# The last stage of a fused decoder kernel: expert slots worked out and filled in two halves, and a tail by batch that stores the output itself

## The reference, cut to the last stage

```python
h = _layernorm(x, ln_g, ln_b).reshape(Tn, D)            # Tn = 1024, D = 128
top_vals, top_idx = jax.lax.top_k(h @ Wr, 2)            # 7 routed experts
gates = jax.nn.softmax(top_vals, axis=-1)
idx, gat = top_idx.T.reshape(-1), gates.T.reshape(-1)   # all first picks, then all second picks
tok = jnp.tile(jnp.arange(Tn), 2)
onehot = jax.nn.one_hot(idx, 7, dtype=jnp.int32)
pos = jnp.sum(jnp.cumsum(onehot, axis=0) * onehot, axis=-1) - 1
keep = pos < CAPACITY                                   # 366
pos_c = jnp.where(keep, pos, CAPACITY)
xe = jnp.zeros((7, CAPACITY, D)).at[idx, pos_c].set(h[tok], mode='drop')
ye = einsum(silu(einsum(xe, W1)) * einsum(xe, W3), W2)  # per expert, 512 wide inside
out_slots = ye[idx, clip(pos_c)] * (gat * keep)[:, None]
routed = jnp.zeros((Tn, D)).at[tok].add(out_slots)
shared = (silu(h @ W1s) * (h @ W3s)) @ W2s
x = _layernorm(x + routed + shared)                     # the kernel's output
```

## Time and profile before

| what | us |
|---|---|
| median of 3 runs (lowest, highest) | 2411.19 (2404.15, 2413.72) |
| the profiled execution's own time | 2407.47 |
| its span, first to last instruction | 2405.6 |
| last stage within it | 2251.8 to 2405.6 |
| PE busy over the span | 2038.5 (85%) |
| mean granted PE clock over the span | 0.906 |

### The profile page before, as it was taken

How to read it: one execution, slowest core, us unless ns; L and a number is a source line. 1 busy time by engine, 2 the same in 40 slices (tenths; PEclk the granted TensorE clock), 3 DMA queues, 4 the chain that set the end, 5 groups by cost and what they waited for, 6 DMA issues and landing times. The chain is left out here.

```text
span 2405.6 us, 59384 instructions
## 1 busy us (share of the span) xinstructions
PE 2038.5 (85%) x24530; PEld 1251.5 (52%) x24530; DVE 1331.8 (55%) x3370; ACT 1129.3 (47%) x2591; POOL 969.7 (40%) x868
## 2 busy tenths in 40 slices
PE   4988999869976899999999999999769756699773
PEld 2445666635543555565555555555535545355452
DVE  3545554447725776767776767776236423465322
ACT  1333445115523676767676767676415211145221
POOL 2010000011215887878787878787110133100123
PEclk8999999879968999999999999999769767889887
DMA  2110000000002021211111212121000032100411
GB/s 66 24 36 1 1 1 1 1 18 3 3 1 72 18 60 27 47 39 42 40 47 35 60 27 51 36 48 24 14 14 7 1 110 89 27 2 2 132 39 40
DMA packets 70558, 78.47 MB, mean 33 GB/s; under 512 B 10608, under 2 KB 48634, under 8 KB 70291
## 3 DMA queue, kind: packets, MB, share of 16 engines
q1 hardware_dynamic: 64098, 61.75, 9.9%
q0 software_dynamic: 3696, 10.56, 1.5%
q10 hardware_dynamic: 2496, 2.36, 0.4%
HBM read 40.90 MB, written 6.82 MB: 20 GB/s over the span
## 5 line engine op out<-in xcount | busy, mean ns | idle before, releaser
L3490 POOL TENSOR_TENSOR l1fb_rinv<-l1fb_ssq,neghalf 128x8 f32<-128x8 f32 x192 | 316.2, 1647 | 159.5 <-DVE l1fb_ssq L3533 157.0
L3633 ACT ACTIVATE l1fb_p<-ps,l1fb_shift 128x64 f32<-128x64 f32 x768 | 177.7, 315 | 158.7 <-PE ps L3789 137.8
L3492 POOL TENSOR_TENSOR l1fb_qk<-l1fb_qk,l1fb_r 128x512 f32<-128x512 f32 x192 | 244.5, 1273 | 0.0
L3696 PE MATMUL ps<-l1fb_wqkv,l1fb_xs 128*128 128x512 f32 x384 | 219.5, 655 | 10.3 <-DVE l1fb_r L3543 6.2
L3494 POOL TENSOR_TENSOR l1fb_qk<-l1fb_qk,l1fb_rinv 128x512 f32<-128x512 f32 x192 | 200.4, 1044 | 15.1
L3543 DVE TENSOR_TENSOR l1fb_r<-ps,l1fb_turn_tab 128x256 f32<-128x256 f32 x384 | 143.0, 414 | 0.0
L3540 DVE TENSOR_TENSOR l1fb_qk<-ps,l1fb_turn_tab 128x512 f32<-128x512 f32 x192 | 132.4, 690 | 14.4 <-POOL l1fb_qk L3492 12.5
L3531 DVE TENSOR_REDUCE l1fb_ssq<-l1fb_sq 128x8 f32<-128x512 f32 x192 | 129.8, 676 | 3.0 <-ACT l1fb_sq L3613 3.0
L3613 ACT ACTIVATE l1fb_sq<-ps 128x512 f32<-128x512 f32 x192 | 118.7, 618 | 11.9 <-PE ps L3696 11.2
L3727 PE MATMUL ps<-ident,l1fb_qk 128*128 128x128 f32 x768 | 116.6, 275 | 5.7 <-POOL l1fb_qk L3494 2.5
L3641 ACT ACTIVATE l1fb_both<-ps 128x512 f32<-128x512 f32 (+1 forms) x194 | 117.3, 605 | 8.3 <-PE ps L3789 7.7
(11 more groups left out here) (722 smaller groups left out, 4773.8 us busy)
## 6 DMA issues: line engine op xcount, KB each, us to landing
l1fb_v<-l1fb_v SPq DMA_DIRECT2D x48, 260.0 KB, 4.2
l1fb_v<-l1fb_v SPq DMA_DIRECT2D x48, 195.0 KB, 4.0
l1fb_wqkv<-in_L_ffn_Wqkv SPq DMA_DIRECT2D x24, 256.0 KB, 2.8
l3f_w<-in_L_ffn_W SPq DMA_DIRECT2D x21, 256.0 KB, 6.5
l1fb_wqkv<-in_L_ffn_Wqkv SPq DMA_DIRECT2D x6, 512.0 KB, 4.7
l1fb_wo<-in_L_ffn_Wo SPq DMA_DIRECT2D x6, 512.0 KB, 4.1
l1fb_w<-in_L_ffn_W SPq DMA_DIRECT2D x6, 341.0 KB, 3.0
l3f_xs<-zeros SPq DMA_DIRECT2D x1, 1344.0 KB, 6.9
```

The lines of the kernel that those rows point to most:

```text
L3490: nc.gpsimd.tensor_tensor(w.rinv[:, u, :], w.ssq[:, u, :], chip.neghalf[:, 0:8], ALU.pow).then_inc(*w.unit_norm.end(f"rinv{u}"))
L3492: nc.gpsimd.tensor_tensor(w.qk[:, u, :], w.qk[:, u, :], fp(w.r2), ALU.add).then_inc(*w.unit_norm.end(f"add{u}"))
L3633: last = nc.scalar.activation(w.p[:, c % 2, q, j, :], ps[:, SCORE_BANK + j, q * SEEN:(q + 1) * SEEN], ACT.Exp, bias=w.shift[:, c, j, q:q + 1])
L3696: nc.tensor.matmul(ps[:, PROJ_BANK(u), :], w.xs[:, x.odd, q * P:(q + 1) * P], w.wqkv[:, col:col + 512], start=True, stop=True)\
```

## The change

It touches `l3_ffn` and the last block of the program only.

1. **Gate.** The 1024 columns of `hT` are made in two halves, the first by DVE once 4 tiles have been turned, the second by ACT. The logits of the first 4 tiles wait for the first half alone. The clearing of the two PSUM banks moves to the head of PE's list, ahead of everything.
2. **Counts.** PE counts first picks as soon as they exist, and second picks after those, two matmuls of 56 columns each time; both stand ahead of the shared expert's first piece.
3. **Placing** is a function `placed(s)`, called for first picks (s = 0) and second picks (s = 1). The 15 successive additions are replaced by three additions over 63 columns (each tile with the one 1, 2 and 4 places before it) on a padded tile `run`, which POOL sets to zero. The second half adds the first half's total. `placed(0)` stands ahead of `mixed(0)`, `placed(1)` between `mixed(0)` and `mixed(1)`.
4. **Scatter.** POOL issues the 8 scatters of first picks when `sent0` is there, the other 8 after `sent1`.
5. **Tail.** DVE adds residual and shared result once (`kepty`, 1024 columns) before the gathers land; it then takes each batch from gathered rows to variance when they arrive. POOL raises the first three batches together (6 columns) and the last alone. All eight normalisations stand at the end of DVE's list, six and then two.
6. **Output.** SP stores three batches after the six, the last batch after the two, within the stage's own block; the extra block is gone.

```diff
+            nc.gpsimd.memset(fp(run), 0.0).then_inc(*rpool.end("runs"))
             eng.wait_ge(*emptied.of(0))
-            eng.wait_ge(*cdve.done("sent"))
             for i in range(2 * TILES):
+                if i % TILES == 0:
+                    eng.wait_ge(*cdve.done(f"sent{i // TILES}"))
                 nc.gpsimd.indirect_dma_start(xs, ...)
...
+            def placed(s):
+                at = slice(s * TILES, (s + 1) * TILES)
+                bank = (5, 4)[s]
+                n = TILES
+                a0, a1 = run[:, 0, s, :, :], run[:, 1, s, :, :]
+                eng.wait_ge(*cpe.done(f"counts{s}"))
+                eng.wait_ge(*rpool.done("runs"))
+                nc.vector.tensor_copy(a0[:, n + 1:2 * n + 1, :], ps[:, bank, S:S + n * E]...)
+                for src, dst, step, before, name in ((a0, a1, 1, "run", "two"), (a1, a0, 2, "two", "four"), (a0, a1, 4, "four", "eight")):
+                    eng.wait_ge(*cdve.done(f"{before}{s}"))
+                    nc.vector.tensor_tensor(dst[:, n:2 * n + 1, :], src[:, n:2 * n + 1, :], src[:, n - step:2 * n + 1 - step, :], ALU.add)
...
+            placed(0)
             mixed(0)
-            totals = ps[:, 5, S:S + 2 * TILES * E].rearrange("p (i e) -> p i e", e=E)
-            for i in range(1, 2 * TILES):
-                nc.vector.tensor_tensor(offs[:, i, :], offs[:, i - 1, :], totals[:, i - 1, :], ALU.add)
-                if i == TILES:
-                    mixed(1)
...
+            placed(1)
+            mixed(1)
             mixed(2)
...
+            nc.vector.tensor_tensor(fp(kepty), ps[:, 6:8, :]..., x_tiles, ALU.add).then_inc(*bdve.end("kept"))
...
+            for which, part in (("", range(0, TILES - QT)), ("_last", range(TILES - QT, TILES))):
+                eng.wait_ge(*bpool.done("rstd" + which))
+                for q in part:
+                    last = nc.vector.tensor_scalar(x_tiles[:, q, :], mixedy[:, q, :], ymv[:, q, 0:1], yroot[:, q:q + 1], ALU.subtract, ALU.mult)
+                last.then_inc(*bdve.end("normed" + which))
...
+            sp.wait_ge(*bdve.done("normed"))
+            sp.dma_start(batch(0, B - 1), chip.x_tok[:, 0:B - 1, :, :]).then_inc(written, 16)
+            sp.wait_ge(*bdve.done("normed_last"))
+            sp.dma_start(batch(B - 1, 1), chip.x_tok[:, B - 1:B, :, :]).then_inc(written, 16)
+            sp.wait_ge(written, 32)
...
-        stored = ctx.enter_context(nc.semaphore("stored"))
-        with nc.Block() as block:
-            @block.sync
-            def _(sp):
-                sp.dma_start(out.rearrange("b (t p) d -> p b t d", p=P), fp(chip.x_tok)).then_inc(stored, 16)
-                sp.wait_ge(stored, 16)
```

163 lines of the change are left out of this document (96 added, 67 removed).

## The result

The changed kernel took **2395.66 us** (median of 11 runs, 2388.5 to 2403.1), the kernel before 2413.36 us beside it (11 runs). The ratio is **0.9927, 95% interval 0.9908 to 0.9946**: 17.6 us less, 13 to 22 by the interval.

What follows compares the result with a forecast made beforehand. Bound: the last stage's path of gate, placing, 16 scatters, load, experts, store, gathers, tail, output. 9.8 + 4.6 = 14.4 us off 2407.47 gives 2393.1, plus 3.7 for the median 2396.8; predicted between, 2395.5, range 2388 to 2403.

Steps and rivals of the forecast that it cites:

- Gate: Gate in halves at the start of the last stage: logits end 1.5 us earlier.
- Placing and scatter: First picks' destinations ready 9.8 us earlier, second picks' with 4.6 us of cover; last scatter ends 9.8 us earlier.
- scatters are held up beside the weights: Scatter stream stands until 2276.5 while the weights load: loss 5.5 us, gain 8.9, time 2401; chance 0.10.
- The clears: PSUM clearing on PE (3.78 us), moved to the stage's start, ends before `z` is there: free.
- The sum: 9.8 us up to the last scatter plus 4.6 us in the tail: 14.4 us saved.
- Experts and clock: PE waits 3.8 to 4.7 us for the first expert's rows; same expert instructions, 64 us; clock falls again.
- The rival with the clock: Clock stays up through the shortened wait ahead of the experts: up to 2.6 us more, time 2393; chance 0.22.
- The cover of 4 us: PE's slack between the shared expert's end and the first expert's rows: 3.8 to 4.7 us, where there were 13.7.
- a sign of being wrong: Ahead of the routed experts: wrong if PE is still on the shared expert when the rows arrive.
- Tail: After the last gather: last normalisation 1.8 us closer, then 3 us to the end instead of 5.9; 4.6 us saved.
- the rule that I weighed: In the tail, DVE's normalisations could shut POOL out of a shared port pair: end about 1 us later.
- the rival of a weaker tail: A block's end costs the same wherever it stands: gain 12.1 or 11.4 us, time 2398; chance 0.11.

Runs made afterwards that it cites:

- four scatters: Changed kernel with only four of the 16 scatters, the loads of the experts' rows waiting for the fourth; stage 131.7 us.
- front: Kernel before with the change's gate, counts, placing and scatters by halves, old tail and output; ratio 0.9988 (0.9966 to 1.0009).
- tail: Kernel before with the tail by batch and the stores in the stage, old gate and placing; ratio 0.9997 (0.9984 to 1.0010).
- after, again: Changed kernel run once more without edit, against the kernel before; ratio 0.9953 (0.9936 to 0.9970), stage 141.4 us.
- both additions: Changed kernel with clears behind the logits, three unread matmuls at stage start, five ahead of the first expert; ratio 0.9937 (0.9918 to 0.9957).
- after: Changed kernel in its first timing, against the kernel before; 2395.66 us, ratio 0.9927 (0.9908 to 0.9946).
- start only: Changed kernel with three unread matmuls at stage start in place of the clears, which go behind the logits; ratio 0.9944 (0.9923 to 0.9965).
- front, again: Kernel before with only gate, counts, placing and scatters by halves, timed a second time; ratio 0.9956 (0.9939 to 0.9972).

## Why the prediction was right, point by point

**Gate.** Logits end 12.15 us from the stage's start instead of 13.55: 1.4 us earlier, forecast 1.5. DVE's half took 0.81 (bounds 0.67 to 0.81), ACT's 0.78, hidden. POOL's memset (476 columns, 0.50 us) cost nothing.

**Placing and scatter.** `sent0` is ready 9.9 us earlier (18.1 us from the start for 28.0), forecast 9.8; `placed(0)` took 2.88 us, forecast 2.95. `sent1` came at 2286.77, and POOL wanted it at 2291.7: cover 4.9, forecast 4.6. The last scatter ended 9.9 us earlier. The rival "scatters are held up beside the weights" fell: they were issued 1.28 us apart in the mean, beside a DMA share of 1.10 in the five microseconds from the first on.

**The clears.** I had them as free. They are free where they stand now, and worth 1.7 us against the old place. The sum was right since it took PE's counts of first picks as done by the second pick, which rests on this move; the step should have said so.

**Experts and clock.** PE waited 4.79 us for the first expert (forecast 3.8 to 4.7), and the clock fell in that wait, as it had in the two of the earlier trace rows. The stretch at 0.66 above shows it, and the experts took 64.1 us. The rival with the clock was priced 0.3 us too high (2.3 measured with four scatters, 64.1 less 61.8), and did not come in this trace.

**What the prediction missed.** The cover of 4 us was taken as fixed. In the second trace the shared expert filled it and 4.4 us more (first expert at 47.5 instead of 43.1). That is a sign of being wrong that the prediction names itself, PE still on the shared expert when the rows arrive: in one of the two traces of the changed kernel it was PE, and not the rows, that ended last ahead of the experts. The other terms hold in both. The delay cost only 2.5 us in the end, since without a wait the clock stays up. PE as the bound ahead of the experts should have been a rival, at the price of its delay less 2.3 us of clock. Signs stood in before's trace: its last silu started 0.3 us after its matmuls' end, where the other seven started with it, and DVE's last product of the shared expert started 2.4 us after PE's row of the accumulation for which it waits (end 2291.22) and 2.35 after the silu (end 2291.26). Timeline of the kernel before:

```profile
2290.66 0.60 ACT L3082 ACTIVATE l3f_act<-ps 128x512 f32<-128x512 f32 x1 [2.32 <-PE ps L3126]
...
2293.61 0.69 DVE L2978 TENSOR_TENSOR l3f_mid<-ps,l3f_act 128x512 f32<-128x512 f32 x1 [3.61 <-remote]
```

**Tail.** 5.0 us (14.6 to 9.6 from the last gather), forecast 4.6. The last batch's variance was there 0.2 us earlier than I had it, the last normalisation 0.5 (eight of them back to back in 2.11 us, POOL's two steps under them), and from there to the end it took 3.12 us, forecast 3.1. POOL's power ran in 0.70 us under DVE's normalisations; in the kernel before, the first of the two took 0.70 with DVE idle and the second 0.71 beside DVE. By the rule that I weighed (the Trainium skill, page "SBUF — State Buffer", section "Who interferes with whom") it could have had to wait; these rows don't show that. So the rival of a weaker tail fell too.

**The median.** 14.4 us off the profiled time, plus the place of the profile among the runs, gave 2395.5. The two timings of the changed kernel gave gains of 17.6 (13 to 22) and 11.3 (7 to 15) us: the sum lies in both, and no single timing could have confirmed its 14.4 to better than 4 us. The hit of 2395.5 on 2395.66 is two misses that cancel: the forecast started in effect from 2409.9 (2395.5 + 14.4), 3.5 below the 2413.36 that before took beside the changed kernel, and between the medians lie 17.7 us, 3.3 more than the sum. The sum itself is carried by the traces: 14.9 us, 9.8 of them up to the end of the last gather and 5.0 behind it, and 12.3 in the second trace.

**What stays open.** What delays PE's announcements is not settled. Shown: among the disturbed executions it follows the scatters; one program shows it in one execution and not in another; and it goes together with lost records of semaphore updates. Those are lost in the ninth stage and beside the gathers too (166 of 256 landings recorded in the changed kernel's second trace), where no scatter of this stage runs. Not shown: that a kernel without scatters beside PE would be free of it in a disturbed execution, since the two that could have shown this ran in a session without the disturbance. One reading is that the recording itself falls behind and holds the updates up. The Trainium skill knows such a thing: page "NOTIFIC — the notification-queue block", section "Overflow: three behaviours, one of which stalls the engine", says that the block which writes these records can discard new ones when their ring is full, and that inside the block the producer is held back rather than a record lost. No run here shows that this is what happened. The other reading is that the landings of the scatters crowd the way on which PE's updates travel, and that the records only suffer with them. No kernel ran that tells the two apart.

Whether the timed runs have the delay is not known either. The four timings whose trace had it gave 2.9 (front), 0.7 (tail), 11.3 (after, again) and 15.2 us (both additions), against 9.8, 4.6, 14.4 and 14.4 of the sum; the three whose trace had none gave 17.6 (after), 13.5 (start only) and 10.6 (front, again) against 14.4, 14.4 and 9.8. The four fall short by 3.3 us in the mean, the three are 1.0 above. That leans to yes, but the shortfall is nearly all of one session: front and tail are 6.9 and 3.9 us short, and both were timed in the first session, against the same executions of before; the two of the second session, equally disturbed in their traces, are 3.1 short and 0.8 above. The tail alone, whose trace hides the delay under a wait, should not be short at all. So the session may be the cause, and not the delay; no run separates them.

No version ran that beats the changed kernel by more than a measurement can tell.

## What to carry to other kernels

Before you shorten a wait, ask what it hides on the other engines and how much that varies: here the change left 4.8 us of 13.7, and beside the earlier scatters the shared expert's last group started up to 12.8 us late in some executions. When an engine's row names another that is waiting itself, compare the time at which the semaphore was raised with the end of the row that raised it. And take a second trace of the same program before you explain a few microseconds between two programs: here it showed that the pauses are not a matter of the code. Before you call such a thing absent in a kernel, make sure that its execution was of the kind that has it: the count of landings in an unchanged stage tells.

## What the runs showed of the hardware that I had not expected

- Beside the scatters ACT's wait on PE's matmuls can end up to 8.0 us after the end of their rows, and the same program may show none of it in another execution. With scatters from 17.4 to 20.7 us on, the first expert then starts at 47.5 to 50.9 us from the start instead of 43.1.
- In those executions the trace keeps 39 to 84 of 256 semaphore landings of the scatters, and 99 to 111 of 128 in the ninth stage; in the others all of them.
- The wait of 4.8 us ahead of the experts costs 2.3 us of clock on top. An engine that fills it by working later loses less than it seems, since the clock stays at 2.4 GHz (the experts in 61.8 us at 1.00 against 64.1 at 0.96).
- The same program, timed twice, gave 0.9988 (0.9966 to 1.0009) and 0.9956 (0.9939 to 0.9972). The two intervals overlap by 0.0006 only, so one timing's interval may be too narrow for what differs between sessions.
- A store inside the stage's block instead of a block behind it saves 2.7 us from the last normalisation to the end (3.1 against 5.8).
